# Last sequence's shared expert: inner products after the expert tiles, outer products in a third PSUM bank of the combining pass; a new order at the end of the first pass

## The chip, the cores and the metric

The kernel runs on one core of one Trainium2 chip. The metric is device time in microseconds (us); lower is better. Three runs of the kernel before give a median of 1098.8 us (1096.66 to 1099.21).

## The reference

Input x is 16 sequences of 512 tokens by 256 channels, float32. The kernel computes two residual blocks:

```
x = x + LN(attn(LN(x)))          # WKV attention: k, v, r projections of a shifted mix, a scan over time, Wo
x = x + LN(moe(LN(x)))
moe(t): logits = t @ gate_w.T + gate_b;  softmax;  top 2 of 8 experts, weights
        y = sum over the 2 chosen experts of  weight * ((silu(t@w1.T+b1) * (t@w3.T+b3)) @ w2.T + b2)   # 256 inner
        z = (silu(t@ws1.T+bs1) * (t@ws3.T+bs3)) @ ws2.T + bs2      # shared expert, 512 inner, every token
        return y + z
```

Matrix products are made of three products of float32r parts (high·high, low·high, high·low).

## The kernel before, in words

Three passes follow each other, each its own block; at the end of a block all engines drain and wait for one another, so the next block begins when the last of them has drained.

**First pass** (`first_pass`): a software pipeline over the 16 sequences; in step i the attention of sequence i, the projection of i-1, routing and the shared expert's inner products of i-2 and its outer products of i-3 stand side by side. Each engine has its own list, written out in its `body`, and for the end in its `finish` (THIRD, SECOND, LAST are sequences 13, 14, 15). DVE does scans, reciprocals (`invert`, L1134), `gate` (L1142), layernorm moments, routing (`rank_experts`, `read_counts`, `place`), the product h (`product`, `late_product`, L1170/L1398) and low parts. ACT does exponentials, silu, high parts and the normalising; GpSimd (POOL) the running sums (`running_sums`, L1545/L1547), low part of g (`g_low`, L1553), the residual addition (`add_x`, L1563), 1/std (`inverse_std`) and the scattering of normalised rows to the experts' slots (`send`, L1577). The chain of the last sequence is: scans → reciprocals → g → `project` (L601) → `normalise_o` → `add_x` → `normalise_x1` → `late_turn_xf` → `late_route` → rank → `late_count` → `place` → `expert_ends`, `tile_bounds`, `tile_tables` (which expert and which slots each of the 71 tiles of 256 rows has) → SyncE (SP) loads rows and weights of the first tiles (`first_rows` L95, `first_weights` L103). The shared expert's output of each sequence is stored to `sum_y` in HBM. For the last sequence its inner products (4 x 12 matmuls of 512 columns, `late_inner`) and outer products (2 x 24 matmuls of 256 columns, `late_outer`) run at the end of this pass, between and behind the routing work; the four products h and four low parts of that sequence stand in DVE's list around the tile tables. SP interleaves the last stores to `sum_y` with the loads of the first tiles. Eight scatters of zeros to spare rows (`begin_scatters`, L1585) end POOL's list; they give the semaphores of the expert pass their first counts.

**Expert pass** (`expert_tiles`): 71 tiles; TensorE has 24 inner, 12 outer matmuls of 256 columns and 4 transposes a tile, POOL adds each tile's rows to `sum_y` by two indirect DMAs.

**Combining pass** (`combine`): 16 tiles of 512 tokens. SP loads the accumulated rows (`acc`) and the residual (`x1`) into four buffers each; TensorE turns the gates (4 transposes) and multiplies them with the output biases (4 matmuls, L2068) into one of two PSUM banks `b_ps`; DVE adds (L2112) and takes moments; POOL, ACT normalise; POOL adds x1 (L2152); ACT stores. A new `acc` load waits for `normed` of three tiles before, the load of `x1` for `res_ready` of three tiles before.

## Time and profile before

| | |
|---|---|
| three runs, median | 1098.8 us (1096.66 to 1099.21) |
| the profiled execution | 1104.38 us, its span 1102.6 us, so 1.8 us lie around the span |
| TensorE / DVE / ACT / POOL busy | 978.8 / 877.7 / 560.8 / 749.0 us |
| first pass ends, expert pass ends (from the timeline) | 666.0 us, 1027.0 us |
| combining pass | 1027.0 us to the end |

The share of busy time is an average over three passes with different limits, so each pass is to be read by itself: which engine or transfer ends its last wait. The times in the timeline are from the start of the span. "SPq" is SyncE's own queue, in which only the issuing of transfers is seen; "idle before" in brackets names who ended the wait. The profiled execution is 5.6 us above the median of the three runs.

### The profile page before, as it was taken

What the parts mean: (1) busy time and instruction counts of PE and PEld (TensorE: products, weight loads), DVE (VectorE), ACT (ScalarE), POOL (GpSimd) and SP (SyncE); (2) the same over time, 40 slices, a digit from 0 to 9 for tenths busy, and PEclk for the clock granted to TensorE, in tenths of its full rate; (3) what the DMA queues carried; (4) which work ended last, traced back from release to release, by engine and by line L of the source; (5) the groups of instructions that cost most, each with busy time, mean ns of one, the idle gap of its engine ahead of it and who ended that gap; (6) DMA issues with size and microseconds to landing.
All of it is one profiled execution on the core that took longest, in us unless ns stands there. A gap on an engine that the chain in (4) does not pass through costs nothing. (4 is left out here: it accounts for less than half of the span.)

```text
span 1102.6 us, 23267 instructions
## 1 busy us (share of the span) xinstructions
PE 978.8 (89%) x6344; PEld 875.6 (79%) x6344; DVE 877.7 (80%) x2255; ACT 560.8 (51%) x1020; POOL 749.0 (68%) x762
## 2 busy tenths in 40 slices
PE   3659899999999999999998978999999999998552
PEld 2547788888888888888887768999999899998331
DVE  6798899999999999999988555777776677676586
ACT  4354475557555755575556523444444444443365
POOL 2353777777777777777776772767766676767488
PEclk9779999999999999999999998999999999999555
DMA  6232442454245424542441465987778968985797
GB/s 198 67 85 85 133 130 97 145 162 129 95 145 161 129 95 143 163 129 95 148 140 59 145 203 164 223 219 120 115 148 178 223 108 222 223 205 82 248 394 286
DMA packets 107893, 171.93 MB, mean 156 GB/s; under 512 B 13869, under 2 KB 75976, under 8 KB 107592
## 3 DMA queue, kind: packets, MB, share of 16 engines
q1 hardware_dynamic: 76120, 119.68, 34.2%
q0 software_dynamic: 26976, 35.93, 18.6%
q10 hardware_dynamic: 4752, 15.80, 3.6%
q8 instruction: 19, 0.31, 0.1%
q14 instruction: 26, 0.21, 0.1%
HBM read 173.53 MB, written 76.08 MB: 226 GB/s over the span
## 5 line engine op out<-in xcount | busy, mean ns | idle before, releaser
L1972 POOL DMA_INDIRECT sum_y<-e_y,e_row_at x142 | 224.7, 1582 | 43.6 <-issue 38.7
L1806 PE MATMUL e_h_ps<-e_z_hi,w_room 128*128 128x256 f32 x1136 | 215.2, 282 | 10.6 <-DMA w_room<-w_split 8.2
L1806 PEld LDWEIGHTS e_h_ps<-e_z_hi,w_room 128*128 128x128 f32 x1136 | 179.8, 189 | 14.3 <-issue 10.0
L1850 ACT ACTIVATE e_act_h<-e_h_ps,w_room 128x256 f32<-128x256 f32 x142 | 67.5, 476 | 190.2 <-PE e_h_ps L1806 145.6
L1806 PE MATMUL e_h_ps<-e_z_lo,w_room 128*128 128x256 f32 x568 | 159.0, 280 | 0.0
L1577 POOL DMA_INDIRECT slots_x<-f_xf,f_at x120 | 129.3, 1077 | 28.8 <-issue 28.6
L1822 PE MATMUL e_y_ps<-w_room,e_h_hi 128*128 128x256 f32 x568 | 117.9, 291 | 1.1 <-DVE e_h_lo L1896 1.1
L1889 DVE SCALAR_TENSOR_TENSOR e_h<-e_h_ps,w_room,e_act_h 128x256 f32<-128x256 f32 x142 | 68.1, 482 | 61.3 <-ACT e_act_h L1850 46.0
L1134 DVE RECIPROCAL f_den<-f_den 128x256 f32<-128x256 f32 (+1 forms) x49 | 109.2, 2234 | 0.5
L1806 PEld LDWEIGHTS e_h_ps<-e_z_lo,w_room 128*128 128x128 f32 x568 | 107.4, 189 | 0.0
L655 PE MATMUL f_h_ps<-f_f_hi,f_w_hi 128*128 128x512 f32 x224 | 92.8, 414 | 5.6 <-DVE f_h_room L1170 3.3
L1822 PEld LDWEIGHTS e_y_ps<-w_room,e_h_hi 128*128 128x128 f32 x568 | 92.2, 189 | 1.3 <-DVE e_h_lo L1896 1.3
L655 PE MATMUL f_h_ps<-f_f_lo,f_w_hi 128*128 128x512 f32 x224 | 88.4, 395 | 0.0
L655 PE MATMUL f_h_ps<-f_f_hi,f_w_lo 128*128 128x512 f32 x224 | 88.1, 393 | 0.0
L1545 POOL TENSOR_TENSOR f_num<-f_num,f_a_sum 128x512 f32<-128x512 f32 x32 | 41.9, 1309 | 66.5 <-DVE f_a_sum L1117 66.5
L1822 PE MATMUL e_y_ps<-w_room,e_h_lo 128*128 128x256 f32 x284 | 79.8, 281 | 0.0
L34 POOL TENSOR_TENSOR e_scratch<-e_scratch 128x1 f32<-128x1 f32 x71 | 23.8, 336 | 74.1 <-DMA sum_y<-e_y,e_row_at 36.4
L582 PE MATMUL f_k_ps<-f_z_hi,w_room 128*128 128x512 f32 x128 | 56.9, 445 | 12.9 <-issue 10.1
L827 ACT ACTIVATE rows_room<-f_k_ps 128x512 f32<-128x512 f32 x32 | 19.1, 598 | 94.3 <-PE f_r_ps L582 94.3
L1563 POOL TENSOR_TENSOR f_x_room<-f_on,f_x_res 128x1024 f32<-128x1024 f32 x16 | 38.5, 2406 | 40.4 <-ACT f_on L872 40.3
L1553 POOL TENSOR_TENSOR f_g_lo<-f_g,f_g_hi 128x512 fp32r<-128x512 f32 x32 | 41.4, 1295 | 33.8 <-ACT f_g_hi L866 33.6
L1114 DVE TENSOR_TENSOR_SCAN f_b_sum<-f_ew,rows_room 128x512 f32<-128x512 f32 x32 | 62.9, 1967 | 0.0
(299 smaller groups left out, 3020.0 us busy)
## 6 DMA issues: line engine op xcount, KB each, us to landing
w_room<-w_split SPq DMA_DIRECT2D x73, 512.0 KB
w_room<-w_split SPq DMA_DIRECT2D x71, 514.0 KB
w_room<-w_split ACTq DMA_DIRECT2D x69, 512.0 KB
rows_room<-slots_x SPq DMA_DIRECT2D x71, 260.0 KB
f_x_in<-x SPq DMA_DIRECT2D x16, 512.0 KB, 5.2
f_x_res<-x SPq DMA_DIRECT2D x16, 512.0 KB, 4.5
x_dram<-f_x_room SPq DMA_DIRECT2D x16, 512.0 KB, 2.9
c_acc<-sum_y SPq DMA_DIRECT2D x16, 512.0 KB, 7.4
```

What stands on the lines that cost most here:

```text
L582: last = pe.matmul(out[:, :], w[:, which, part, c * P:(c + 1) * P], z, start=(part == HERE and n == 0), stop=(part == SHIFT and n == 2))
L655: last = pe.matmul(out[:, :], a[:, which, c, q * P:(q + 1) * P], b[p][:, c, :], start=(n == 0), stop=(n == 5))
L1114: dve.tensor_tensor_scan(b_sum[c][:, 1:T + 1], ew[:, c:c + 1].to_broadcast([P, T]), ek[c][:, :], 0.0, ALU.mult, ALU.add)
L1134: dve.reciprocal(den[c][:, at], den[c][:, at]).then_inc(rec_ready, 1)
L1545: pool.tensor_tensor(num[c][:, :], num[c][:, :], a_sum[c][:, 0:T], ALU.add)
L1553: pool.tensor_tensor(g_lo[:, c, :], g[c][:, :], g_hi[:, c, :].bitcast(F32), ALU.subtract)\
L1577: pool.indirect_dma_start(out=slots_x[:, :], out_offset=bass.IndirectOffsetOnAxis(ap=at[p][:, j, k:k + 1], axis=0), in_=xf_of(s, p)[:, j, ...
L1806: last = pe.matmul(h_ps[q][:, which, :], w13(p, q, part)[:, which, c, :], z[p % 2][:, c, :], start=(n == 0), stop=(n == 5))
L1822: last = pe.matmul(y_ps[p % 2][:, j, :], a[p % 2][:, q, j * P:(j + 1) * P], w2(p, part)[:, q, :], start=(n == 0), stop=(n == 3 * parts - 1))
L1850: act.activation(act_h[q][:, :], h_ps[q][:, 0, :], ACT.Silu, bias=bias(p, 0, q)).then_inc(silu_ready, 1)
L1889: dve.scalar_tensor_tensor(out=h[p % 2][:, q, :], in0=h_ps[q][:, 1, :], scalar=bias(p, 1, q), in1=act_h[q][:, :], op0=ALU.add, op1=ALU.mul ...
L1972: pool.indirect_dma_start(out=dst[:, :], out_offset=bass.IndirectOffsetOnAxis(ap=row_at[p][:, j:j + 1], axis=0), in_=y[p][:, j, :], in_off ...
```

## The change

1. The shared weights, biases, f parts and five semaphores of the shared expert are allocated outside the first pass and live on. The LAST sequence's `late_inner`, `late_silu`, `late_product`, `late_h_high`, `late_low_h` leave `finish` and become `shared_inner`, `shared_silu`, `shared_product`, `shared_h_high`, `shared_h_low` at the end of the lists of the expert pass (after the last tile, into the PSUM tensors `h_ps` and `turn_ps`).
2. Its outer products become `outer` inside `combine`: a third `b_ps` takes biases and outer products of tile 15, which TensorE does fourth (ORDER = 0, 1, 2, 15, 3, 4 ...). DVE still goes 0 to 15. `gt` has three buffers instead of two.
3. The rows of the last sequence in `sum_y` get zeros by one DMA early (L486 of the new file) instead of two stores of y at the end.
4. `begin_scatters` moves from the end of POOL's `finish` into step 0 of its `body` (two pairs, with zeros of `y[0]`), `spare_rows` to DVE's start. `read_y` of step 0 waits for them.
5. `finish` of TensorE, ACT, DVE and POOL is put in another order; SP issues `first_weights(0)` first, then rows 0, rows 1, weights 1, rows 2, rows 3, then the two stores of SECOND.

```diff
@@ first_pass, SP @@
+            sp.dma_start(by_tiles(shared_y[LAST * T:SEQS * T, :]), nobody[:, :, 0:C].to_broadcast([P, SUBS, C]))\
+                .then_inc(late_zeros_stored, 16)
...
-            late_store_y(SECOND, 0)
...
+            first_weights(0)
             sp.wait_ge(cleared, 16 * (E + 1))
...
             first_rows(0)
-            first_weights(0)
             first_rows(1)
-            late_store_y(SECOND, 1)
+            first_weights(1)
             first_rows(2)
-            late_store_y(LAST, 0)
-            first_weights(1)
-            late_store_y(LAST, 1)
             first_rows(3)
-            sp.wait_ge(late_y_stored, 32)
+            store_y(SECOND, 0)
+            store_y(SECOND, 1)
+            sp.wait_ge(late_zeros_stored, 16)
@@ first_pass, TensorE, finish @@
                 inner(THIRD, 1, 2)
+                project(LAST)
                 inner(THIRD, 1, 3)
                 late_turn_xf(SECOND)
-                project(LAST)
                 late_route(SECOND)
                 late_outer(THIRD, 0)
                 late_count(SECOND)
                 late_inner(SECOND, 0)
                 late_outer(THIRD, 1)
+                late_turn_xf(LAST)
                 late_inner(SECOND, 1)
+                late_route(LAST)
                 late_inner(SECOND, 2)
-                late_turn_xf(LAST)
+                late_count(LAST)
                 late_inner(SECOND, 3)
-                late_route(LAST)
-                late_inner(LAST, 0)
-                late_count(LAST)
                 late_outer(SECOND, 0)
-                late_inner(LAST, 1)
-                late_inner(LAST, 2)
-                late_inner(LAST, 3)
                 late_outer(SECOND, 1)
-                late_outer(LAST, 0)
-                late_outer(LAST, 1)
@@ first_pass, POOL, finish @@
                 running_sums(LAST, 0)
-                send(THIRD - 1, 0, 1, (1, 2, 3))
+                send(THIRD - 1, 0, 1, (1,))
                 inverse_std(LN_O, SECOND, 0)
+                send(THIRD - 1, 0, 1, (2, 3))
+                make_nobody()
+                running_sums(LAST, 1)
+                pool.wait_ge(g_ready, 2 * LAST + 1)
                 add_x(SECOND, 0)
-                running_sums(LAST, 1)
                 g_low(LAST, 0)
+                g_low(LAST, 1)
                 inverse_std(LN_X1, SECOND, 0)
...
                 send(THIRD, 1, 0, (0, 1))
+                inverse_std(LN_O, LAST, 1)
+                h_low(THIRD, 2)
+                send(THIRD, 1, 0, (2,))
+                add_x(LAST, 1)
                 h_low(THIRD, 3)
-                send(THIRD, 1, 0, (2, 3))
-                inverse_std(LN_O, LAST, 1)
-                send(THIRD, 1, 1, (0, 1))
-                add_x(LAST, 1)
-                send(THIRD, 1, 1, (2, 3))
+                send(THIRD, 1, 0, (3,))
                 inverse_std(LN_X1, LAST, 1)
+                send(THIRD, 1, 1, (0, 1, 2, 3))
...
-                for p in range(4):
-                    begin_scatters(p)
@@ expert_tiles, TensorE (ACT and DVE alike: silu, product, high, low of four q) @@
+            def shared_inner(q):
+                for which, to, read in ((0, s_banks(q)[0], s_silu_ready), (1, s_banks(q)[1], s_h_ready)):
+                    wait(pe, read, DONE + q - 1 if q >= 2 else 0)
+                    n = 0
+                    for c in range(CC):
+                        for a, b in ((s_w13["hi"], f_hi), (s_w13["hi"], f_lo), (s_w13["lo"], f_hi)):
+                            last = pe.matmul(to, a[:, which, c, q * P:(q + 1) * P], b[:, c, :], start=(n == 0), stop=(n == 5))
+                            n += 1
+                last.then_inc(s_inner_done, 1)
+
             steps_by_four(pe, body, -2, *LOOP, tiles + 1)
+            pe.wait_ge(h_ready, tiles * parts)
+            pe.wait_ge(zlo_ready, tiles)
+            for q in range(Q):
+                shared_inner(q)
@@ combine @@
+        ORDER = [*range(3), LAST, *range(3, LAST)]
...
+            def bias(n):
+                s = ORDER[n]
+                pe.wait_ge(gt_ready, n + 1)
+                if s == LAST:
+                    pe.wait_ge(hlo_ready, 2 * Q)
+                else:
+                    wait(pe, summed, s - 1)
                 for j in range(SUBS):
+                    last = pe.matmul(bank_of(s)[:, j, :], rows_of(gt[n % 3][:, :], j), b_out[:, :], start=True, stop=s != LAST)
+                    if s == LAST:
+                        last = outer(bank_of(s)[:, j, :], j)
                 last.then_inc(b_done, 1)
...
+                for q in range(Q):
+                    for a, b in ((h_hi, w2["hi"]), (h_lo, w2["hi"]), (h_hi, w2["lo"])):
+                        n += 1
+                        last = pe.matmul(to, rows_of(a[:, q, :], j), b[:, q, :], start=False, stop=n == 3 * Q)
...
             def add(s):
-                dve.wait_ge(b_done, s + 1)
+                dve.wait_ge(b_done, ORDER.index(s) + 1)
```

**The order on DVE, end of the first pass, from the last sequence's second scan to its second g** (f_den, f_num and f_g are the denominators, numerators and g; f_h_room is h of the shared expert; f_x_room is x1). Before:

```order
L1117 SCALAR_TENSOR_TENSOR f_a_sum<-f_ew,f_ekv 128x512
L1170 SCALAR_TENSOR_TENSOR f_h_room<-f_h_ps,f_bias,f_h_room 128x512
L1134 RECIPROCAL f_den<-f_den 128x256 x2
L1142 TENSOR_TENSOR f_g<-f_num,f_den 128x512
L1081 BN_STATS f_stats<-f_x_room 128x6 x4
L1170 SCALAR_TENSOR_TENSOR f_h_room<-f_h_ps,f_bias,f_h_room 128x512
L1091 BN_AGGR f_totals<-f_stats 128x2 x4
L1126 SCALAR_TENSOR_TENSOR f_den<-rows_room,f_den 128x512
L1134 RECIPROCAL f_den<-f_den 128x256
L1178 TENSOR_TENSOR f_h_lo<-f_h_room,f_h_hi 128x512 x2
L1170 SCALAR_TENSOR_TENSOR f_h_room<-f_h_ps,f_bias,f_h_room 128x512
L1134 RECIPROCAL f_den<-f_den 128x256
```

And now:

```order
L1075 SCALAR_TENSOR_TENSOR f_a_sum<-f_ew,f_ekv 128x512
L1092 RECIPROCAL f_den<-f_den 128x256
L1128 SCALAR_TENSOR_TENSOR f_h_room<-f_h_ps,f_bias,f_h_room 128x512
L1084 SCALAR_TENSOR_TENSOR f_den<-rows_room,f_den 128x512
L1100 TENSOR_TENSOR f_g<-f_num,f_den 128x512
L1092 RECIPROCAL f_den<-f_den 128x256
L1128 SCALAR_TENSOR_TENSOR f_h_room<-f_h_ps,f_bias,f_h_room 128x512
L1092 RECIPROCAL f_den<-f_den 128x256
L1100 TENSOR_TENSOR f_g<-f_num,f_den 128x512
```

One half reciprocal went ahead of the scan, and the moments of x1, the two low parts of h and one h went behind the second g.

**The order on SP, from the last clearing of slot tails to the end of the first pass** (w_split holds the expert weights, slots_x the rows, rows_room and w_room their places in SBUF). Before, the loads with the stores between them:

```order
L509 DMA sum_y<-f_x_res 128x2x256
L94 TENSOR_LOAD tile_slot
...
L95 DMA rows_room<-slots_x 128x520
...
L103 DMA w_room<-w_split 128x1024
L103 ISA
L103 DMA w_room<-w_split 128x1028
L103 ISA
L103 DMA w_room<-w_split 128x1024
...
L95 DMA rows_room<-slots_x 128x520
L509 DMA sum_y<-f_x_res 128x2x256
```

And now its beginning and its end:

```order
L101 TENSOR_LOAD tile_expert
L101 ISA x2
L103 ISA
L103 DMA w_room<-w_split 128x1024
...
L95 DMA rows_room<-slots_x 128x520
L427 DMA sum_y<-f_y 128x2x256 x2
```

Four stores stood ahead of or between the loads; now two stand behind them.

**The order on TensorE, start of the combining pass**, now (c_gt_ps: turned gates; s_h_hi, s_h_lo: h of the last sequence; before, only rows of the first two kinds stand here):

```order
L2085 MATMUL c_gt_ps<-eye,c_gates 27x128 x4
L2096 MATMUL c_b_ps<-c_b_out,c_gt 128x256 x4
L2085 MATMUL c_gt_ps<-eye,c_gates 27x128 x4
L2096 MATMUL c_b_ps<-c_b_out,c_gt 128x256
L2107 MATMUL c_b_ps<-f_w_hi,s_h_hi 128x256
L2107 MATMUL c_b_ps<-f_w_hi,s_h_lo 128x256
L2107 MATMUL c_b_ps<-f_w_lo,s_h_hi 128x256
```

Four groups of one bias matmul and twelve outer matmuls stand between the biases of tile 2 and those of tile 3.

## Rows read from the trace of the kernel before

**Rows 1.** Windows: busy us (instructions) of PE, PEld, DVE, ACT, POOL, PEclk, DMA, GB/s.
```profile
575.00:666.00 91.00, 73.61 (x442) 64.00 (x441) 57.55 (x192) 39.81 (x72) 59.95 (x67) 0.96 0.44 143
1031.00:1035.00 4.00, 4.00 (x16) 2.92 (x16) 3.81 (x12) 0.59 (x1) 0.40 (x1) 0.50 1.03 414
1027.00:1103.00 76.00, 36.35 (x128) 24.50 (x128) 56.56 (x176) 42.52 (x80) 56.48 (x49) 0.50 0.88 332
```

**Rows 2.** DVE timeline, second scan to second g: start us, length us, line, work.
```profile
582.77 1.20 DVE L1117 TENSOR_TENSOR_SCAN f_a_sum<-f_ew,f_ekv 128x512 f32<-128x512 f32 x1
596.24 1.74 DVE L1134 RECIPROCAL f_den<-f_den 128x256 f32<-128x256 f32 x1
598.02 1.03 DVE L1142 TENSOR_TENSOR f_g<-f_num,f_den 128x512 f32<-128x512 f32 x1
```

**Rows 3.** POOL timeline: the last g_low, h_low of THIRD, and the last add_x.
```profile
599.79 1.27 POOL L1553 TENSOR_TENSOR f_g_lo<-f_g,f_g_hi 128x512 fp32r<-128x512 f32 x1 [1.29 <-ACT f_g_hi L866]
604.16 1.28 POOL L1569 TENSOR_TENSOR f_h_lo<-f_h_room,f_h_hi 128x512 fp32r<-128x512 f32 x1
612.97 2.39 POOL L1563 TENSOR_TENSOR f_x_room<-f_on,f_x_res 128x1024 f32<-128x1024 f32 x1
```

**Rows 4.** TensorE timeline: matmuls after a thin stretch, at the low and the full clock.
```profile
644.09 0.53 PE L727 MATMUL f_turn_ps<-f_f_hi,f_w_hi 128*128 128x512 f32 x1 [1.86 <-issue]
646.55 0.41 PE L751 MATMUL f_k_ps<-f_w_hi,f_h_hi 128*128 128x256 f32 x1
646.76 0.41 PE L751 MATMUL f_k_ps<-f_w_hi,f_h_lo 128*128 128x256 f32 x1
648.08 0.28 PE L751 MATMUL f_k_ps<-f_w_lo,f_h_hi 128*128 128x256 f32 x1
648.20 0.28 PE L751 MATMUL f_k_ps<-f_w_hi,f_h_hi 128*128 128x256 f32 x1
```

**Rows 5.** ACT timeline: normalise_x1 of the last sequence.
```profile
619.86 2.08 ACT L872 ACTIVATE rows_room<-f_x_room,f_offset,f_rstd 128x256 f32<-128x256 f32 x4 [2.30 <-POOL f_offset L55]
```

**Rows 6.** DVE timeline: last routing, first and last step of the tile tables.
```profile
629.21 0.19 DVE L1189 TENSOR_TENSOR f_lg<-f_v_ps,f_gate_bias 128x32 f32<-128x32 f32 x1 [0.84 <-PE f_v_ps L703]
649.57 0.74 DVE L1334 TENSOR_REDUCE f_num<-f_x_in 128x71 f32<-128x568 f32 x1
652.49 0.22 DVE L1347 SCALAR_TENSOR_TENSOR tile_land<-f_num,f_land_base 1x70 int32<-1x70 f32 x1
```

**Rows 7.** SP's issues: clearing, first rows, last rows; and its wait at the end.
```profile
636.59 10.92 SPq L430 DMA_DIRECT2D slots_x<-f_x_in  x8
653.47 0.38 SPq L95 DMA_DIRECT2D rows_room<-slots_x  x1
663.35 0.33 SPq L95 DMA_DIRECT2D rows_room<-slots_x  x1
SPq L142 <- DMA sum_y<-f_x_res: 1.2, 1, 1.2
```

**Rows 8.** Ends of the expert pass: last matmul, POOL's drain (count, length ns, start).
```profile
1015.63 0.28 PE L1822 MATMUL e_y_ps<-w_room,e_h_hi 128*128 128x256 f32 x1
L1663 POOLq DRAIN  x1: 8027/8027/8027, 1018.7 to 1018.7; - x1
```

**Rows 9.** Combining pass: TensorE's biases of tile 2, DVE's additions of tiles 3 and 9.
```profile
1033.30 1.31 PE L2068 MATMUL c_b_ps<-c_b_out,c_gt 27*128 27x256 f32 x4
1041.39 1.21 DVE L2112 TENSOR_TENSOR c_acc<-c_b_ps,c_acc 128x1024 f32<-128x1024 f32 x1
1065.96 1.23 DVE L2112 TENSOR_TENSOR c_acc<-c_b_ps,c_acc 128x1024 f32<-128x1024 f32 x1 [1.80 <-DMA c_acc<-sum_y]
```

**Rows 10.** POOL timeline in step 0: the two gaps that take scatters; one scatter's length.
```profile
41.43 1.90 POOL L1545 TENSOR_TENSOR f_num<-f_num,f_a_sum 128x512 f32<-128x512 f32 x1 [7.42 <-DVE f_a_sum L1117]
52.18 1.30 POOL L1553 TENSOR_TENSOR f_g_lo<-f_g,f_g_hi 128x512 fp32r<-128x512 f32 x1 [6.41 <-ACT f_g_hi L866]
655.23 1.31 POOL L1585 DMA_INDIRECT sum_y<-f_x_in,f_spare_at  x1 [0.30 <-issue]
```

More of the change, by code:

```diff
@@ L367, in first_pass @@
         held = sem("held")
-        sent = [sem(f"sent{p}") for p in range(2)]
+        sent = early["sent"]
         CONSTS = 12
@@ L739, in late_outer @@
                 else:
[L740 to L743 removed]
+                    pe.wait_ge(late_hlo_ready, Q)
+                    if half == 0:
+                        pe.wait_ge(y_read, 2 * s)
                     out = late_y_ps[half]
@@ L931, in read_y @@
                     act.wait_ge(y_stored[half], 16 * s)
+                elif half == 0:
+                    for p in range(4):
+                        act.wait_ge(early["y_stored"][p], 16 * PAIR)
                 act.activation(y[half][:, :, :], y_ps, ACT.Copy).then_inc(y_read, 1)
@@ L1417, in finish @@
                 denominator(LAST, 0)
+                invert(LAST, 0, slice(0, T // 2))
                 read_counts(THIRD)
                 scans(LAST, 1)
+                invert(LAST, 0, slice(T // 2, T))
                 product(THIRD, 0)
-                invert(LAST, 0, slice(0, T // 2))
-                invert(LAST, 0, slice(T // 2, T))
+                denominator(LAST, 1)
                 gate(LAST, 0, 2)
-                moments_x1(SECOND, 0)
+                invert(LAST, 1, slice(0, T // 2))
                 product(THIRD, 1)
-                aggregate(LN_X1, SECOND, 0)
-                denominator(LAST, 1)
-                invert(LAST, 1, slice(0, T // 2))
-                first_h_low(THIRD, 0)
-                first_h_low(THIRD, 1)
-                product(THIRD, 2)
                 invert(LAST, 1, slice(T // 2, T))
@@ L1434, in finish @@
                 place(THIRD, 1)
-                late_f_low(SECOND)
-                product(THIRD, 3)
+                moments_x1(SECOND, 0)
+                aggregate(LN_X1, SECOND, 0)
+                product(THIRD, 2)
+                first_h_low(THIRD, 0)
+                first_h_low(THIRD, 1)
                 moments_o(LAST, 1)
                 aggregate(LN_O, LAST, 1)
+                low_w(LAST)
+                product(THIRD, 3)
+                late_f_low(SECOND)
+                moments_x1(LAST, 1)
+                aggregate(LN_X1, LAST, 1)
                 add_gate_bias(SECOND, late_logits_ps)
@@ L1690, in expert_tiles @@
         scratch = sb("scratch", [P, 2])
+        shared = early["shared"]
+        s_w13, s_bias, f_hi, f_lo = (shared[n] for n in ("w13", "bias", "f_hi", "f_lo"))
+        s_h_hi, s_h_lo = shared["h_hi"], shared["h_lo"]
+        Q, S_T = s_h_hi.shape[1], s_h_hi.shape[2]
+        s_act_h = [sb(f"s_act_h{p}", [P, S_T]) for p in range(2)]
+        s_h = [sb(f"s_h{q}", [P, S_T]) for q in range(Q)]
         b_raw = sb("b_raw", [G, C])
@@ L1985, in _, with combine @@
             steps_by_four(pool, body, 0, *LOOP, tiles + 2)
-def combine(nc, acc_dram, x1_dram, ahead, out):
+def combine(nc, acc_dram, x1_dram, ahead, shared, out):
     C = acc_dram.shape[1]
@@ L2005, in combine @@
         minus_half = sb("minus_half", [P, SUBS])
-        gt = [sb(f"gt{p}", [G, T], F32R) for p in range(2)]
+        w2, h_hi, h_lo, hlo_ready = shared["w2"], shared["h_hi"], shared["h_lo"], shared["late_hlo_ready"]
+        Q, LAST = w2["hi"].shape[1], tiles - 1
+        ORDER = [*range(3), LAST, *range(3, LAST)]
+        gt = [sb(f"gt{p}", [G, T], F32R) for p in range(3)]
         acc = [sb(f"acc{p}", [P, SUBS, C]) for p in range(DEPTH)]
@@ L2099, in store @@
                 act.dma_start(rows(out, s), res[s % DEPTH][:, :, :]).then_inc(stored[s % DEPTH], 16)
-            for i in range(-2, tiles + 2):
-                gates_turned(i + 2)
+            for i in range(-3, tiles + 2):
+                gates_turned(i + 3)
                 normalise(i)
```

224 lines of the change are left out of this document (112 added, 112 removed).

## The prediction

> **What bounds the kernel now.** I read the page first. TensorE is busy for 89% and DVE for 80% of the span, but that is a mean over three passes, so the busy time by windows comes next. In the reader's eye should be two stretches in which no engine is at its limit: the end of the first pass, where TensorE works 73.6 of 91 us and DVE 57.6 of 91, and the combining pass, where TensorE works half the time at a granted clock of 0.50 (the lower level, 1.2 GHz) and the DMA engines are at 0.88 [rows 1]. There a chain of single operations sets the time. The steady part of the first pass and the 350 us of the tiles keep their lists, so they cost nothing either way. Then I read the timeline of each engine across the three ends.
>
> End of the first pass: SP loads the first rows and weights only after DVE has the tile tables, and the next pass starts when SP and POOL have drained. The tables start at 649.57 and are done at 652.7 [rows 6]. SP issues the first rows at 653.47, the last at 663.35 to 663.7, then waits 1.2 us for a late store [rows 7]. The expert pass starts at 666.0.
>
> End of the expert pass: the last matmul ends at 1015.9. POOL's drain, 8.03 us from 1018.7, ends at 1026.7 [rows 8], and the combining pass starts at 1027.0. So TensorE stands still for 11 us.
>
> **Part 1, the chain of the last sequence, walked anew.** All times on the clock of the trace.
> - *To the projection.* DVE's second scan still ends at 583.97 [rows 2], since it waits for ACT's exponentials. Behind it now stand one half reciprocal, h, the denominator, g, half, h, half, g. At 1.74 a half [rows 2] and 0.7 to 0.95 for each of the others that is 9.1 us: 593.1. Before, g ended at 599.05 [rows 2]. ACT and POOL add the same 0.7 and 1.3 as before, so project(LAST) starts at 595.2 instead of 601.1 [rows 3]: 5.9 us earlier. TensorE is free there, since inner(THIRD, 3) went behind it.
> - *To x1.* The projection takes 2.9 (598.1), moments and their aggregate 2.4 (600.5). POOL sends two rows of THIRD first, so its 1/std ends at 603.2. ACT normalises to 605.1, POOL has h_low and a send in hand until 605.6, and add_x (2.39) ends at 608.0. Before: 615.4 [rows 3]. That is 7.4 earlier.
> - *What is late next.* POOL's h_low(THIRD, 3) now stands behind that add_x and ends at 609.3 instead of 605.4 [rows 3]. late_outer(THIRD, 0) waits for it, and late_count(SECOND), late_inner(SECOND, 0), late_outer(THIRD, 1) and the transposes of the last sequence are queued behind it on TensorE. TensorE has only the thin routing matmuls between 602 and 609.3. After such a stretch the trace shows the low clock: at 644.09, after a wait of 1.86 us, matmuls of 256 columns stand 0.21 us apart, and at 648.1, 4 us of work later, 0.12 us [rows 4]. I take the low clock: 24 x 0.21 = 5.1 instead of 2.9 us, end 614.5. Then ACT reads y (615.2) and normalises (2.2, [rows 5]) to 617.4, instead of 622.0. TensorE meanwhile does count 0.6, inner 2.9, outer 2.9, so its transposes end at 622.0; inner(SECOND, 1) 2.8 and route 1.7 give logits at 626.6. Before: 629.21 [rows 6]. So 2.6 us are left of the 7.4, or 4.9 with the clock up.
> - *To the tables.* Ranking 2.4, then two table loads of ACT (1.3 each) and its high part hold DVE until 630.5; counts and place 1.9, 632.4. expert_ends 1.7, one h and its low part with a wait 2.1, tile_bounds 4.0, one more h and low 2.0: the tables start at 642.3. Before, the four h and four low parts of the last sequence stood here too, start 649.57 [rows 6]. 7.3 us earlier, done at 645.4.
> - *SP.* From the tables' end to the last rows' issue it was 11.0 us (652.7 to 663.7, [rows 7]). The three stores between the loads (0.5 each and their gaps) go, two come behind: 9.7. And SP waits for no fresh store, which gives 1.2 [rows 7]. Start of the expert pass 645.4 + 9.7 + 0.5 = 655.6: **10.4 us earlier**. POOL's list ends by 644, its eight scatters having left.
>
> The Trainium skill (TensorE: Matmul & The Clock Gate, section Why this matters for your kernels) says to leave TensorE no idle gaps in mid-kernel, because its clock then falls to the lower level. By that rule the price is the 2.3 us taken above; without a fall the gain would be 12.7.
>
> **Part 2, moved to step 0.** POOL's first gap there is 7.42 us, four scatters take 4 x (1.31 + 0.30) = 6.4; 1/std uses none of it. The second gap is 6.41 us, again 6.4 [rows 10]. The g_low behind it may start 0.3 us later, and TensorE takes it only at 55.2, 1.7 us after it is done. Cost 0, bounds 0 and 0.5. The spare rows on DVE (0.6) lie in a wait of 1.65 us. The zero stores of 512 KB replace as many bytes.
>
> **Part 3, the drain.** shared_inner is 48 matmuls of 512 columns. Two of 256 at the full clock are 2 x 0.12 [rows 4], so 0.23 each and 10.95 together: 1015.8 to 1026.9. Then silu 0.7, product 0.75, high 0.65 and low 0.7 of the last q: 1029.8. The old end is 1026.7, POOL's drain [rows 8], which goes on beside it. So the start of the combining pass is **3.1 us later**. Bounds: 2.5 and 5.
>
> **Part 4, the combining pass.** Call its start t0 (1027.0 before). TensorE ends the biases of tile 2 at 1034.6 [rows 9], turns four more gates and comes to tile 15 at t0 + 8.5. DVE wants tile 3 at 1041.4, t0 + 14.4 [rows 9]. Between lie the new block L and then one turn and four bias matmuls, 2.2 us. L is 48 x 0.21 and four biases at 0.3: 11.3 us at the low clock, 6.3 at the full one. The clock was 0.50 here with TensorE busy 4.00 of 4.00 us [rows 1], but on narrow work; full-width work got it back after 4 us [rows 4]. I take that: 4.5 us low, the rest full, L = 8.3. Tile 3 is ready at t0 + 19.0 less 0.6, DVE stands 4.0 us. Ends: 1.4 (full clock) and 7.6 (low throughout). Some of it comes back: DVE later waits 1.8 us for tile 9 and twice more for acc rows, 4.1 in all (the first in [rows 9]), because the DMA queues are full; a DVE that is late asks later. But they idle in part of the stall, since four buffers are all that is loaded ahead. I take 1.8 back: **2.2 us** (0 to 7.6).
>
> **Sum**: -10.4 + 0 + 3.1 + 2.2 = -5.1 on the profiled 1104.38 us, whose span is 1102.6 and which is 5.6 above the median. Put on the median of 1098.8: 1093.7, say **1094**. What a measurement of this kernel tells from no change is 0.3%, 3.3 us.
>
> **The rivals.**
> - *A, forecast (0.42)*: 1094, its own range 1091 to 1097.
> - *B, no clock fall (0.25)*: the clock stays up over TensorE's thin stretch at 602 to 609 (for: the thin matmuls of route; against: [rows 4]), and is soon back in the combining pass. 2.3 and 1.6 less: 1090.
> - *C, the clearing of slot tails binds (0.20)*: SP's eight clears take 10.92 us and began 7.4 us after the logits [rows 6, 7]. Now they begin near 633.5 and end at 644.4, 1 us before the tables; the first rows also wait for their landing. If place or the landing slips, 1 to 4 us of the gain go: 1096.5. For: DMA share near 1 there. Against: 1 us of room, and the weights go first.
> - *D, slower: the block of tile 15 stalls DVE (0.13)*. Its stationary operand is read with a stride of four, as that of the bias matmuls, of which four take 1.31 us [rows 9], 0.31 each. If that is the step of all 52, L = 16.1, tile 3 is ready at t0 + 26.8 and DVE stands 12.4 us. Everything behind shifts, nothing comes back: -10.4 + 3.1 + 12.4 = +5.1, 1103.9. It decides from L of 14.3 us on (then -7.3 + 10.6 = 3.3). Against: the 1.31 holds the 0.44 length of the last matmul, which leaves 0.29 as the step, and the work is at the low clock.
>
> By the same page of the Trainium skill the clock comes back once TensorE is kept busy; by that rule B's combining pass holds. The 0.50 at 4.00 of 4.00 us [rows 1] speaks against it for narrow work.
>
> **Numbers.** Faster by over 3.3 us is below 1095.5: 0.34 of A, all of B, 0.01 of C: 0.60. Within: 0.08 of A, 0.19 of C, 0.01 of D: 0.28. Slower: 0.12. The range 1088.5 to 1101 holds A, B and C and leaves out D and the outermost of B.
>
> **What would show it.** Right: project(LAST) near 595, logits near 626.6, tables done near 645.4, expert pass starting at 655 to 656; combining pass 14 to 15 us after the last tile's last matmul; DVE's idle time before the addition of tile 3 about 4 us, ended by TensorE. Wrong: an SP queue that waits for the clears, a stall at tile 3 beyond 8 us, a step 0 that ends later, or a pace of the tiles other than before.

## The result, and the profile after

The changed kernel takes 1111.5 us at the median (1105.4 to 1111.9, 5 runs), the kernel before 1098.8 (1096.7 to 1101.5): ratio 1.0102, 95% interval 1.0085 to 1.012, some 11 us **slower**. The forecast was 1094, and its range ended at 1101. The profiled execution has a span of 1110.1 us.

Where the stretches begin and end, in the traces of before (the one of [rows 1 to 10]), of a second execution of the kernel before (run b0_before_again), and of the change. Each boundary is a row of a timeline: DVE's last scan, TensorE's first turn of the tiles, the last tile's last matmul, the first turn of the combining pass.

| | before | before, second | changed | forecast for the change |
|---|---|---|---|---|
| last scan of the first pass | 582.8 | 579.6 | 582.3 | no change |
| from there to the tiles | 83.2 | 83.4 | 76.0 | -10.4 |
| tiles, to their last matmul | 349.6 | 349.2 | 353.0 | no change |
| to the combining pass | 11.4 | 11.6 | 14.7 | +3.1 |
| combining pass | 75.5 | 73.8 | 84.0 | +2.2 |
| span | 1102.6 | 1097.7 | 1110.1 | -5.1 |

The second trace of before corrects the first: that one had lost 3 us early (its seventh scan starts at 131.6 us, the second trace's at 128.6). In four of five traces of kernels in the old order the last scan starts at 579.3 to 579.7 us. So the change is 2.7 us late before its new code at the end of the pass begins.

**Combining pass.** TensorE's timeline in the changed kernel, the first outer matmuls of tile 15, two from the third group, the last one, and the biases of tile 3:

```profile
1034.52 0.59 PE L2096 MATMUL c_b_ps<-c_b_out,c_gt 27*128 27x256 f32 x1
...
1035.44 0.43 PE L2107 MATMUL c_b_ps<-f_w_hi,s_h_lo 128*128 128x256 f32 x1
1035.68 0.44 PE L2107 MATMUL c_b_ps<-f_w_lo,s_h_hi 128*128 128x256 f32 x1
...
1043.16 0.40 PE L2107 MATMUL c_b_ps<-f_w_hi,s_h_hi 128*128 128x256 f32 x1
1043.40 0.40 PE L2107 MATMUL c_b_ps<-f_w_hi,s_h_lo 128*128 128x256 f32 x1
...
1048.47 0.39 PE L2107 MATMUL c_b_ps<-f_w_lo,s_h_hi 128*128 128x256 f32 x1
...
1049.23 1.21 PE L2096 MATMUL c_b_ps<-c_b_out,c_gt 27*128 27x256 f32 x4
```

The same stretch by windows (busy us and instructions of PE, PEld, DVE, ACT, POOL, then PEclk, DMA share, GB/s):

```profile
1035.00:1042.00 7.00, 7.00 (x27) 6.29 (x26) 4.93 (x19) 4.21 (x9) 5.27 (x6) 0.50 0.77 266
1043.00:1048.00 5.00, 5.00 (x21) 4.74 (x21) 0.00 (x0) 0.00 (x0) 0.80 (x1) 1.00 0.82 320
```

And DVE's additions of tiles 2 and 3:

```profile
1036.22 1.22 DVE L2151 TENSOR_TENSOR c_acc<-c_b_ps,c_acc 128x1024 f32<-128x1024 f32 x1
...
1050.48 1.23 DVE L2151 TENSOR_TENSOR c_acc<-c_b_ps,c_acc 128x1024 f32<-128x1024 f32 x1 [10.38 <-PE c_b_ps L2096]
```

The granted clock (PEclk) rises from 0.50 to 1.00, as forecast, but the matmuls stand 0.24 us apart ahead of that and 0.23 to 0.24 behind it. The block takes 14.2 us (1034.5 to 1048.7) instead of 8.3, and DVE stands 10.4 us instead of 4.0. In the last window the weight loads (PEld, the loading of the stationary operand) are busy 4.74 of 5.00 us. That they set the pace is tested by a2 below.

**End of the first pass.** TensorE: project(LAST), late_outer(THIRD, 0), the first turn of the tiles:

```profile
594.29 0.38 PE L579 MATMUL f_turn_ps<-w_room,f_g_hi 128*128 128x256 f32 x1 [0.85 <-POOL f_g_lo L1501]
...
610.80 0.55 PE L729 MATMUL f_shared_ps<-f_w_hi,f_h_hi 128*128 128x256 f32 x1 [4.02 <-issue]
611.15 0.41 PE L729 MATMUL f_shared_ps<-f_w_hi,f_h_lo 128*128 128x256 f32 x1
...
658.32 1.94 PE L1757 MATMUL e_turn_ps<-eye,rows_room 128*128 128x128 f32 x8 [7.73 <-PEq L142]
```

POOL's last add_x and the h_low behind it:

```profile
607.14 2.35 POOL L1511 TENSOR_TENSOR f_x_room<-f_on,f_x_res 128x1024 f32<-128x1024 f32 x1
609.43 1.27 POOL L1517 TENSOR_TENSOR f_h_lo<-f_h_room,f_h_hi 128x512 fp32r<-128x512 f32 x1
```

DVE: last routing, first and last step of the tables:

```profile
627.59 0.19 DVE L1147 TENSOR_TENSOR f_lg<-f_v_ps,f_gate_bias 128x32 f32<-128x32 f32 x1 [0.21 <-PE f_v_ps L681]
...
643.07 0.74 DVE L1292 TENSOR_REDUCE f_num<-f_x_in 128x71 f32<-128x568 f32 x1
...
645.96 0.22 DVE L1305 SCALAR_TENSOR_TENSOR tile_land<-f_num,f_land_base 1x70 int32<-1x70 f32 x1
```

SP's issues, and from its waits the one for the tables:

```profile
634.50 9.44 SPq L415 DMA_DIRECT2D slots_x<-f_x_in  x8
646.94 2.79 SPq L103 DMA_DIRECT2D w_room<-w_split  x3
650.63 1.43 SPq L95 DMA_DIRECT2D rows_room<-slots_x  x2
652.83 1.36 SPq L103 DMA_DIRECT2D w_room<-w_split  x3
654.94 1.42 SPq L95 DMA_DIRECT2D rows_room<-slots_x  x2
656.40 1.34 SPq L427 DMA_DIRECT2D sum_y<-f_y  x2
```

```profile
SPq L101 <- DVE tile_land L1305: 2.0, 1, 2.0
```

The chain runs as drawn: projection at 594.3 (forecast 595.2), the low clock behind the thin stretch (matmuls of 256 columns 0.21 us apart, granted clock 0.50 from 611 to 613 us), logits 627.6 (626.6), tables done at 646.2 (645.4). SP waits 2.0 us for the tables, so its clearing of slot tails does not bind in this trace (in two later ones it does, see a3). From the tables' end to the tiles it is 12.1 us instead of 10.2: the first three weight loads take 2.79 us to issue, the same three of tile 1 only 1.36. Why the first three take longer is not shown.

**End of the expert pass.** TensorE: last tile's matmul, last of shared_inner, first turn of the combining pass:

```profile
1011.33 0.29 PE L1789 MATMUL e_y_ps<-w_room,e_h_hi 128*128 128x256 f32 x1
...
1022.43 0.39 PE L1807 MATMUL e_turn_ps<-f_f_hi,f_w_lo 128*128 128x512 f32 x1
1026.05 1.88 PE L2085 MATMUL c_gt_ps<-eye,c_gates 128*27 128x128 f32 x8 [3.23 <-PEq L1618]
```

11.2 us of matmuls and 3.2 of chain; 11.0 and 2.9 were forecast. Three effects thus need a cause: the slow block, the late last scan, and tiles that take 3.4 to 3.8 us more although their lists are the same.

### The profile page after: what moved, and what is told of

Read it like the earlier page. It is cut to its first block and busy times, and to the rows that moved or that the text cites. A ratio compares the mean times of both kernels' runs of the same rounds, so it can differ in the third digit from the quotient of the medians.

```text
span 1110.1 us, 23253 instructions
## 1 busy us (share of the span) xinstructions
PE 990.5 (89%) x6344; PEld 888.3 (80%) x6344; DVE 876.7 (79%) x2255; ACT 559.4 (50%) x1018; POOL 753.2 (68%) x763
## 5 line engine op out<-in xcount | busy, mean ns | idle before, releaser
L1773 PE MATMUL e_h_ps<-e_z_hi,w_room 128*128 128x256 f32 x1136 | 219.4, 284 | 9.2 <-DMA w_room<-w_split 8.2
L560 PE MATMUL f_k_ps<-f_z_hi,w_room 128*128 128x512 f32 x128 | 56.5, 442 | 14.8 <-issue 11.9
L1906 DVE TENSOR_SCALAR e_y<-e_y_ps,e_gate 128x256 f32<-128x256 f32 x142 | 61.8, 476 | 1.0 <-PE e_y_ps L1789 1.0
```

What stands on the lines that cost most here:

```text
L560: last = pe.matmul(out[:, :], w[:, which, part, c * P:(c + 1) * P], z, start=(part == HERE and n == 0), stop=(part == SHIFT and n == 2))
L1773: last = pe.matmul(h_ps[q][:, which, :], w13(p, q, part)[:, which, c, :], z[p % 2][:, c, :], start=(n == 0), stop=(n == 5))
L1906: last = dve.tensor_scalar(y[p][:, j, :], y_ps[p % 2][:, j, :], gate[p][:, j:j + 1], None, ALU.mult)
```

## Experiments

Each ratio is to the kernel before on the same chip and has its 95% interval. The first four were planned and run together. Where no ratio is given, the kernel ran once, and only its trace is read.

**a2_rows_together**: h is stored in the order in which the combining pass reads it.

```diff
-  dve.scalar_tensor_tensor(out=s_h[q][:, :], in0=s_banks(q)[1], ...
+  dve.scalar_tensor_tensor(out=s_h[q][:, :].rearrange("g (j p) -> g j p", j=4),
+                           in0=s_banks(q)[1].rearrange("g (p j) -> g j p", j=4), ...
-  last = pe.matmul(to, rows_of(a[:, q, :], j), b[:, q, :], ...
+  last = pe.matmul(to, a[:, q, j * P:(j + 1) * P], b[:, q, :], ...
```

> The changed kernel, with h of the last sequence stored in the order in which the combining pass reads it (DVE reads with the stride instead), so that the stationary operand of the 48 outer matmuls is contiguous. They stood 0.235 us apart in the changed kernel at either clock. Theory 'stride': the strided load sets the step; then 0.21 at the low and 0.12 at the full clock, the block of tile 15 takes 7 to 9 us instead of 14.2, DVE stands 4 to 5 us before tile 3 instead of 10.4, and the time is 5 to 6 us below the changed kernel, near 1106. Rival 'no stride': the step comes from the load of a 128-column float32r operand itself, the block stays at 14 us and the time at 1111.

1.0066 (1.0041 to 1.0092), some 4 us below the changed kernel where 5 to 6 had been expected. Its TensorE, at the low clock and at the full one:

```profile
1039.62 0.41 PE L2110 MATMUL c_b_ps<-f_w_lo,s_h_hi 128*128 128x256 f32 x1
1039.84 0.41 PE L2110 MATMUL c_b_ps<-f_w_hi,s_h_hi 128*128 128x256 f32 x1
...
1042.99 0.28 PE L2110 MATMUL c_b_ps<-f_w_hi,s_h_hi 128*128 128x256 f32 x1
1043.11 0.28 PE L2110 MATMUL c_b_ps<-f_w_hi,s_h_lo 128*128 128x256 f32 x1
```

and its DVE at tile 3:

```profile
1049.57 1.22 DVE L2154 TENSOR_TENSOR c_acc<-c_b_ps,c_acc 128x1024 f32<-128x1024 f32 x1 [4.93 <-PE c_b_ps L2099]
```

The step falls to 0.21 and 0.12 us. The block takes 9.3 us, DVE stands 4.9, the pass takes 77.6 us: 2.1 above the first trace of before and 3.8 above the second, where 2.2 had been forecast. "Stride" stands. The weight loads of this line by shape, changed kernel first, then this one (count, busy us, mean ns, over both clocks):

```profile
L2107 PEld LDWEIGHTS c_b_ps<-f_w_hi,s_h_lo 128*128 128x128 f32 x16 | 5.3, 332 | 0.0
```

```profile
L2110 PEld LDWEIGHTS c_b_ps<-f_w_hi,s_h_lo 128*128 128x128 f32 x16 | 3.6, 224 | 0.0
```

The Trainium skill (SBUF — State Buffer, section Door 1: The DMA port swizzle) says that SBUF is read in lines of 16 bytes, that an access which crosses into a new line pays, and that float32 may be strided by four for free. The stride here is just four, 16 bytes, so every element is in a new line. The trace bears out that such a load costs more, and not that a stride of four is free: 332 against 224 ns. That it is the lines of 16 bytes that cost, no run here shows.

**a3_spread**: the block is cut up, four matmuls behind the biases of each of tiles 2 to 14, still strided.

```diff
-                if s == LAST:
-                    pe.wait_ge(hlo_ready, 2 * Q)
...
+            steps = [(j, n) for j in range(SUBS) for n in range(3 * Q + 1)]
+            for s in range(-1, LAST):
+                turn(s + 1)
+                if s >= 0:
+                    bias(s)
...
+                if s >= FIRST:
+                    for at in range((s - FIRST) * PER, min((s - FIRST + 1) * PER, len(steps))):
+                        last = outer(at)
```

> The changed kernel, with the 52 matmuls of tile 15 spread, four behind the biases of each of tiles 2 to 14 (the turned gates of tile 15 get a buffer of their own), still strided. TensorE waited 1.9 us a tile for the turned gates before; four matmuls take 0.94 us. Theory 'stall': nearly all of the 8.6 us by which the combining pass grew is the one block in front of tile 3; then DVE never waits for TensorE, the pass takes 75.6 to 77 us, and the time is 7 to 9 us below the changed kernel, 1103 to 1104. Rival 'load': the pass has no room for 12 us more of TensorE and each tile gets later; then the pass takes over 80 us and the time stays above 1107.

1.0017 (0.9996 to 1.0038); the pass takes 75.2 us. DVE's one long wait is replaced by seven short ones:

```profile
DVE c_acc L2157 <- PE c_b_ps L2092: 5.7, 7, 1.3
```

This trace, and the one of a2, show something else: the clearing of the slot tails can bind after all. SP's clears, its wait for them, and the end of the tables on DVE:

```profile
632.77 15.30 SPq L415 DMA_DIRECT2D slots_x<-f_x_in  x8
SPq L94 <- DMA slots_x<-f_x_in: 1.3, 1, 1.3
...
644.96 0.22 DVE L1305 SCALAR_TENSOR_TENSOR tile_land<-f_num,f_land_base 1x70 int32<-1x70 f32 x1
```

The clears end at 648.1, 2.9 us behind the tables. In a2 they take 15.25 us and end 2.2 behind them; in the nine other traces with this end of the pass they take 9.4 to 9.6. So a2 and a3 have 78.8 and 78.3 us from the last scan to the tiles. Why the clears took longer in these two is open.

**a4_no_outer**: the outer products of tile 15 are left out, so the last sequence lacks the shared expert's output.

```diff
-                    if s == LAST:
-                        last = outer(bank_of(s)[:, j, :], j)
```

> The changed kernel without the outer products of tile 15 (the last sequence lacks the shared expert's output); the order of the turns and biases stays. Theory 'stall': the combining pass takes the 75.6 us of before, and the time is what the change would cost without its block: 1111.5 - 8.6, some 1103. It is the floor for the run with the spread block. What is above 1098.8 then is the drain (3.2) and the tiles, less the gain at the end of the first pass.

1.0026 (1.0006 to 1.0046), the pass 73.6 us. That is a3's time within the uncertainty: spread, the outer products cost nothing that can be measured, and "stall" holds. But neither is faster than the kernel before, although -7.1 at the end of the first pass and +3.2 behind the tiles would put them 4 us below it.

**a1_before_moved**: the kernel before, its expert pass moved in SBUF.

```diff
+        sb("pad", [P, 12296])
         expert_tiles(nc, TILES, 2, slots_x, sum_y, w_split, ...
```

> The kernel before with 48 KB a partition set aside in front of the expert pass, so that the buffers of that pass lie about where the change puts them; nothing else. In the trace of the change a tile takes 4.71 us in its quiet stretches (4.66 before), and the inner matmuls of the tiles have means of 284 and 283 ns instead of 282 and 280. Theory 'place': the addresses do that; then the tiles here take 353 to 354 us instead of 349.9, the time is 3 to 4 us above the kernel before. Rival 'draw': it differs from one execution to the next; then the time is within 1.5 us of the kernel before, and the tile takes 4.66 us or whatever this execution drew.

1.0033 (1.0012 to 1.0055): an empty buffer costs 3.6 us. In the trace the tiles take 351.4 us (349.2 and 349.6 before; 353 to 354 were expected). "Place" stands, but not what about the place.

**b0_before_again**: no edit.

> The kernel before, unchanged, for a second trace of it: how far its stretches differ from one execution to the next. In the first trace the last sequence's second scan began at 582.8 us, in four traces of changed kernels at 582.1 to 583.1, in the one with moved buffers alone at 579.7. If 582.8 was an ordinary draw, this one has 582 to 583; if a late one, 579 to 580, and then the change costs some 2.5 us ahead of its new end of the first pass too.

One time, 1099.5 us, last scan at 579.6: the first trace was the odd one. DVE's seventh and its last scan, in b0 and in the changed kernel:

```profile
128.61 1.20 DVE L1117 TENSOR_TENSOR_SCAN f_a_sum<-f_ew,f_ekv 128x512 f32<-128x512 f32 x1
...
579.57 1.20 DVE L1117 TENSOR_TENSOR_SCAN f_a_sum<-f_ew,f_ekv 128x512 f32<-128x512 f32 x1
```

```profile
130.15 1.20 DVE L1075 TENSOR_TENSOR_SCAN f_a_sum<-f_ew,f_ekv 128x512 f32<-128x512 f32 x1
...
582.31 1.20 DVE L1075 TENSOR_TENSOR_SCAN f_a_sum<-f_ew,f_ekv 128x512 f32<-128x512 f32 x1
```

1.5 us are there by the seventh scan, 1.2 more come over the 450 us behind it.

**b1_before_32** and **b2_after_32**: `sb("pad", [P, 8])` in front of the expert pass, in the kernel before and in the changed one.

> The kernel before with 32 bytes a partition set aside in front of the expert pass: its buffers for z start at a multiple of 64 bytes, as in the change (before: 32 bytes past one), and 49 KB less far away. Theory 'phase': the place within 64 bytes decides; the tile then takes 4.73 us at the median instead of 4.67 and the kernel 3 to 4 us more, as with 48 KB set aside (ratio 1.0033). Rival 'distance': the pace stays at 4.67 and the time that of the kernel before.

> The changed kernel with 32 bytes a partition set aside in front of the expert pass: its buffers for z start 32 bytes past a multiple of 64, as in the kernel before. Theory 'phase': the tile takes 4.67 us again, the time is 3 to 4 us below the changed kernel, ratio to the kernel before some 1.007 instead of 1.0102. Rival 'distance': 4.73 us and 1.010.

b1: 1.0017 (0.9998 to 1.0035). b2: 1.0102 (1.0072 to 1.0133). To read the pace without the stalls at a change of expert, take the 14 tiles between the 20th and the 34th row of e_gate, a stretch that is quiet in every trace. In b0:

```profile
759.74 0.23 DVE L1925 TENSOR_TENSOR e_gate<-e_more,rows_room 128x2 f32<-128x2 f32 x1
...
824.81 0.16 DVE L1925 TENSOR_TENSOR e_gate<-e_more,rows_room 128x2 f32<-128x2 f32 x1
```

and in the changed kernel:

```profile
756.42 0.23 DVE L1925 TENSOR_TENSOR e_gate<-e_more,rows_room 128x2 f32<-128x2 f32 x1
...
822.41 0.16 DVE L1925 TENSOR_TENSOR e_gate<-e_more,rows_room 128x2 f32<-128x2 f32 x1
```

65.07 / 14 = 4.648 against 65.99 / 14 = 4.714 us. By that measure b1 has 4.714 with only 32 bytes set aside, which rules out "distance", and b2 4.731, which rules out the phase of 64 as I had it. In time, b1's interval reaches down to no change, so there the slower pace shows in the trace and not clearly in the whole.

**b3_best**: a2 and a3 together, the four matmuls now between turn and biases, 32 bytes set aside, the last high and low part of h in the combining pass, and the low part of q 2 ahead of the last product.

> The changed kernel with all that the runs so far point to: h stored in the order in which it is read; the 52 matmuls of tile 15 in fours between the turn and the biases of each tile, where TensorE waited 1.5 us for the turned gates; 32 bytes set aside; the high and low part of the last q of h in the combining pass, while it waits for its first loads (the expert pass ends 1.4 us sooner). Sum against the kernel before, from the traces: end of the first pass -5 to -7, tiles 0, end of the expert pass +1.8, combining pass -1 to 0: -4 to -6 us, ratio 0.995 to 0.997. If the 3 us that the medians of the changed kernels lie above their traces' sums are real, 0.998 to 1.000.

1.0018 (0.9997 to 1.0039): a miss, and no better than a3. The combining pass has 73.2 us, and DVE waits no more for TensorE; the tiles have 4.731 us, and the end of the expert pass 14.8 us as before (see e1).

**c1_four_scatters**: four scatters in step 0 instead of eight.

```diff
-                for j in range(PAIR):
+                for j in range(1):
...
-        BEGUN = 16 * SUBS
+        BEGUN = 16
...
```

> The changed kernel with four scatters in step 0 instead of eight (the counts of the tiles start at 16 instead of 32). In the trace of the change the four in POOL's first gap took 8.1 us instead of the forecast 6.4, so running_sums(0, 1) began 1.7 us late; the second scan of the last sequence came at 582.3 us, against 579.3 to 579.7 in three of four traces of kernels in the order of before. Theory 'scatters': the whole 2.6 us comes from there; the scan is back at 579.5 to 580.5 and the time 2 us below the changed kernel. Rival 'place of f': only some 0.5 to 1 us comes from the scatters, and the rest from step 3 on, where the shared expert first reads the f parts that the change moved; the scan stays at 581.5 or above.

1.0083 (1.0054 to 1.0113). POOL in step 0, in the changed kernel and in c1:

```profile
35.43 1.51 POOL L1534 DMA_INDIRECT sum_y<-f_y,f_spare_at  x1 [0.67 <-issue]
37.24 1.71 POOL L1534 DMA_INDIRECT sum_y<-f_y,f_spare_at  x1 [0.30 <-issue]
39.26 1.93 POOL L1534 DMA_INDIRECT sum_y<-f_y,f_spare_at  x1 [0.30 <-issue]
41.49 1.72 POOL L1534 DMA_INDIRECT sum_y<-f_y,f_spare_at  x1 [0.30 <-issue]
42.77 1.74 POOL L1493 TENSOR_TENSOR f_num<-f_num,f_a_sum 128x512 f32<-128x512 f32 x1
```

```profile
37.46 1.71 POOL L1534 DMA_INDIRECT sum_y<-f_y,f_spare_at  x1 [0.30 <-issue]
41.47 1.89 POOL L1493 TENSOR_TENSOR f_num<-f_num,f_a_sum 128x512 f32<-128x512 f32 x1 [2.30 <-DVE f_a_sum L1075]
```

The scatters take 1.5 to 1.9 us here, not 1.31, and running_sums starts 1.3 us later with four than with two. In c1 the seventh scan stands at 128.46, the last at 580.59, 1.7 us sooner each: "scatters" explains the first 1.5 us, not the 1.2 behind them. The other traces say the same: the seventh scan starts at 129.7 to 131.1 in the ten with eight scatters in step 0, at 128.0 to 128.9 in the three with four (c1, c3, e1), and at 127.9 to 128.6 in the old order, the first trace of before aside. By the ratios alone (1.0083 against 1.0102) the 2 us are not clear of the noise.

**c2_phase** and **c4_zphase_8k**: z and the moved f parts 32 bytes past a multiple of 128, as before; or only the buffers of the expert pass, z first, by 8160 bytes.

```diff
+        phase = [sb("phase0", [P, 24])]
         early["shared"] = {"w13": ...
+        phase.append(sb("phase1", [P, 8]))
...
+        sb("pad", [P, 24])
         expert_tiles(nc, TILES, 2, slots_x, sum_y, w_split, ...
```

> The changed kernel with 96 bytes set aside ahead of the moved f parts (and 32 behind, so that nothing else of the first pass moves) and 96 bytes in front of the expert pass. Both buffers that TensorE reads as the moving operand then start 32 bytes past a multiple of 128, as before; with 0 or 32 bytes set aside they start 64 or 96 past one, and the tiles took 4.73 us both times. Theory 'phase of 128': the tile takes 4.67 us, the tiles 349 to 350 us instead of 353, and the scan of the last sequence comes 1.5 to 2.5 us sooner, since the step from 109.1 to 130.2 us (scans 5 to 6; 19.6 us before) and the 0.1 us more in each later step are the f parts; the time is 4 to 6 us below the changed kernel. Rival 'distance': 4.73 us and no change.

> The changed kernel with 8160 bytes set aside in front of the expert pass: z stands at the same place within 8192 bytes as in the kernel before. If the phase of 128 is the rule, the tile takes 4.67 us here too; if only this one is fast, the place within some larger block decides; if neither, it is the distance from the weights.

4.648 and 4.647 us a tile: the pace of before, at three different distances. c2's ratio is 1.0085 (1.0062 to 1.0109), 2 us below the changed kernel with overlapping intervals, where 4 to 6 had been expected. Its last scan stays at 582.9, so the phase of f does nothing that shows. Its tiles took 354.3 us in spite of the regained pace, with 12.1 us of waits for weights; the table below takes these waits out.

**d1_z_only** and **d2_rest_only**: 96 bytes ahead of z and 32 behind it; or 96 behind z.

> The changed kernel with the four z buffers of the tiles alone 32 bytes past a multiple of 128 (96 bytes set aside ahead of them, 32 behind), h and y where the change has them. If the moving operand of the inner matmuls is what the place matters to, the tile takes 4.67 us; if it is another buffer of the pass, 4.73.

> The reverse: z where the change has it, and all buffers behind it (silu's output, h, its parts, y) moved by 96 bytes to 32 past a multiple of 128. If z decides, 4.73 us a tile; if the rest, 4.67.

The same two rows, of d1:

```profile
760.28 0.23 DVE L1926 TENSOR_TENSOR e_gate<-e_more,rows_room 128x2 f32<-128x2 f32 x1
...
825.27 0.16 DVE L1926 TENSOR_TENSOR e_gate<-e_more,rows_room 128x2 f32<-128x2 f32 x1
```

| z starts past a multiple of 128 by | us a tile | tiles less waits for weights, us | in |
|---|---|---|---|
| 32 bytes | 4.642 to 4.648 | 341.3 to 342.3, d1 344.7 | before, b0, c2, c4, d1, c3, e1 |
| 64 bytes | 4.707 to 4.717 | 343.4 to 345.8 | changed, a1, a2, a3, a4, b1, c1, d2, d3 |
| 96 bytes | 4.731 | 346.6, 347.7 | b2, b3 |

In the pace of the quiet stretch the eighteen executions have no exception, and d1 against d2 shows that it is z. At 0.067 us a tile it is 4.8 us over 71 tiles if no tile hides it, an estimate. The third column is TensorE's time from the first turn of the tiles to the last tile's last matmul, less its waits for the load of weights (w_room from w_split). These waits differ from one execution to the next: 7.3 to 12.4 us at 32 bytes, 6.5 to 12.0 at 64, 5.5 and 5.9 at 96; in the changed kernel and in the first trace of before they are 8.2 both times. So the 3.4 us between those two traces are the pace, while a single tile stretch, or a ratio, can hide or double such an effect. (d1 and d2 took 1116.5 and 1115.8 us, one execution each, and are read for the pace only.)

**d3_before_f_moved**: the kernel before with the allocations of the change alone.

> The kernel before with part 1 of the change alone: weights, biases and one pair of f parts of the shared expert allocated outside the first pass (which moves the other buffers of that pass by 8 KB, and z of the tiles to 64 bytes past a multiple of 128). In the kernel before the last scan comes 451.0 us behind the seventh, in the changed kernels 451.7 to 453 us. Theory 'place of f': 452 here too, and 4.73 us a tile. Rival: it is the new code of step 0 or the lists, then 451.0 here, and 4.73 a tile all the same.

The last scan comes 451.7 us behind the seventh (451.0 in b0, 452.2 in the changed kernel), the tile takes 4.717. So by this one trace 0.7 of the 1.2 us are the moved buffers; which one is open, and so is the rest.

**c3_best**: b3, c1 and c2 together, and SP loads the weights of tile 1 and the rows of tiles 2 and 3 at the start of the expert pass.

```diff
             first_rows(1)
-            first_weights(1)
-            first_rows(2)
-            first_rows(3)
@@ expert_tiles, SP @@
+            load_weights(sp, tile_of, weights, 1, W_ALL, *early["weights"][1])
+            for n in (2, 3):
+                load_rows(sp, tile_of, slots, n, early["rows"][n], early["rows_loaded"][n])
```

> The version with everything: spread and contiguous outer products, four scatters, the 96 + 32 + 96 bytes, the last high and low part of h in the combining pass, and weights of tile 1 and rows of tiles 2 and 3 loaded by SyncE at the start of the expert pass instead of ahead of it (the other engines were drained at 652 us and SyncE at 658). Against b3_best, whose ratio to the kernel before was 1.0018: 4 us at the start of the expert pass, 3.5 in the tiles and 2 in the first pass if the theories above hold: ratio 0.993 to 0.995. If only the start of the expert pass holds: 0.998.

0.9958 (0.9942 to 0.9974): below both kernels, and just short of the 0.993 to 0.995 expected. From the last scan to the tiles 72.1 us, tiles 348.8, combining pass 73.7. From the tables' end to the tiles it is 9.7 us, 11.5 in c1: the loads moved behind the start gave 1.8 us of the 4 expected.

**e1_best**: c3 with the last product unstrided and the low part of q 2 moved behind it, into the combining pass. Against the changed kernel:

```diff
+                if q == Q - 1:
+                    dve.scalar_tensor_tensor(out=s_h[q][:, :], in0=s_banks(q)[1], ...
...
             shared_h_low(1)
             shared_product(3)
-            shared_h_low(2)
-            shared_h_low(3)
```

> c3_best with the low part of the third q behind the block too and the last product unstrided (the high and low part of the last q read with the stride, in the combining pass). In c3_best DVE stood 1.58 us ahead of that low part, which took 0.69, and the product behind it 1.11 us; now the product can begin when silu is done, 0.45 us after 1012.9, and takes 0.75. If this chain sets the end: 13.4 us from the last tile's matmul to the combining pass instead of 14.8, and the combining pass no longer than 73.7 us; ratio 0.9945 instead of 0.9958. If SyncE, POOL or the drain of TensorE sets it, 14.8 as before.

0.9944 (0.9925 to 0.9963), 1093.8 us against 1100.3 of the kernel before beside it. TensorE at the end of the pass:

```profile
1016.38 0.39 PE L1807 MATMUL e_turn_ps<-f_f_hi,f_w_lo 128*128 128x512 f32 x1
1018.60 1.03 PE L2089 MATMUL c_gt_ps<-eye,c_gates 128*27 128x128 f32 x8 [1.83 <-PEq L1615]
```

1.8 us of waiting instead of 3.2, and 13.3 us from the last tile instead of 14.8: the chain of silu and product set that end. In b3 and c3 I had put a low part ahead of the last product, and the 1.4 us were lost waiting for its high part. The combining pass took 75.1 us, not the 73.7 or less expected, and as a whole e1 is not told apart from c3 (0.9944 against 0.9958).

## Why the prediction was wrong

The forecast failed in two steps above all. It priced the 48 outer matmuls of tile 15 at the step of a contiguous stationary operand, and it put the tiles at nothing because their lists stay. The first was worth 6.4 us of the combining pass (84.0 against 77.6 with contiguous h), the second 3.4 us of the tiles.

- **Part 4, +2.2 (0 to 7.6): wrong, +8.5 to +10.2.** L, the block of tile 15, was 14.2 us instead of 8.3, and DVE stood 10.4 us instead of 4.0. The term counted the outer matmuls at the steps of contiguous ones, and wrote the 0.29 of the strided bias matmuls [rows 9] down to the clock. With contiguous h the term comes near: L 9.3, stall 4.9, +2.1 or +3.8 by which trace of before is taken. Rival D had the mechanism and 0.13; its step was 0.31 instead of 0.24, so it stood at 12.4 us of stall where 10.4 came. (D also left out the 0.6 us that the forecast takes off tile 3's time; with it, 11.8.) It ought to have been the bound of the term, since it was the nearest row with that access pattern. D's total of 1103.9 was too low all the same, because it kept the rest of the sum.
- **The tiles, 0: wrong, +3.4 in the profiled execution.** "Keep their lists, so they cost nothing either way" was the failed sentence: the change moved z by 32 bytes against the multiples of 128, and a tile takes 4.714 us instead of 4.645 to 4.648.
- **Part 1, -10.4: right in mechanism, 3.3 too much.** Eleven traces of changed kernels with that end have 74.1 to 78.8 us from the last scan to the tiles, mean 76.4, against 83.5 in five of the old order: -7.1. In the profiled execution the stretch from the last scan to the end of the tables took 1.2 us more than drawn, SP's part 1.9 more. The low clock behind the thin stretch cost what rows 4 said, so rival B's first half is out. Rival C did not come in the profiled execution, where SP waited for the tables and not for its clears; it came in two of the eleven traces, a2 and a3, and without these the mean is 76.0. Its margin was drawn too wide: logits at 626.6 and 7.4 us more give 634.0 for the first clear and not 633.5, which leaves half a microsecond and not 1.
- **Part 2, 0 (0 to 0.5): wrong, 1.5 to 2.** The term took the scatter's 1.31 us from the end of the pass; in the first gap of step 0 it was 1.5 to 1.9, and 6.4 us of work in a gap of 7.42 left no room for that. c1 shows it. A further 1.2 us by the end of the pass had no term; by one trace 0.7 come with the allocations, the rest is open.
- **Part 3, +3.1: right** (3.3 and 3.1 against the two traces of before).
- **The sum.** Against the second trace of before the stretches of the profiled execution add up without a rest: 1.5 + 1.2 up to the last scan, -7.4, tiles +3.8, +3.1, combining pass +10.2, together +12.4, the difference of the spans 1110.1 and 1097.7. The ratio of the many runs gives 11.2. Against the first trace of before it is +7.5 only, because that one was 3 us late of its own by the seventh scan and took 1.7 us more in its combining pass.

## What to carry over

Price a matmul by rows with the same access pattern of its stationary operand: a stride of four float32 made the load 332 ns instead of 224 and took away nearly all that the full clock would have given; store the operand in the order in which it is read. A block of TensorE that the next engine does not need belongs in the gaps between the pieces that it does need, in fours rather than in one. After any change of allocation compare the pace of code that was not touched, and take two traces of the kernel before, since one may be 3 us off.

## What was unexpected of the hardware

The place of the moving operand within 128 bytes moves the pace of a pass bound by TensorE: 4.65, 4.71 and 4.73 us a tile at 32, 64 and 96 bytes. Why is open: a start at a multiple of 128 was not tried, and moving one pair of f parts of the first pass back (c2) showed no such effect. Matmuls of 256 columns whose stationary operand is read with a stride of four stood 0.24 us apart at the granted clock of 0.50 and 0.23 at 1.00, so the full clock gave next to nothing back; with the operand contiguous it was 0.21 and 0.12. The eight clears of slot tails took 9.4 to 9.6 us in nine traces of changed kernels and 15.3 in two.
